# Last attention layer: first adjacency rows masked in the preparation, node softmax moved behind it, weights turned two chunks later

## The reference, cut to what matters

```
h = relu(layernorm(x))
node_att = softmax(h @ node_w, axis=0)         # one number per node, over all nodes
e = (h @ edge_w) @ (h @ edge_w).T              # 2708 x 2708 scores
e = where(adj > 0, e, -9e15)
edge_att = softmax(e, axis=1)
out = adj * (node_att * edge_att) @ (h @ weight) + bias
x = x + out
```

## Time and profile before

| what | value |
|---|---|
| time before, median of 3 runs | 2699.87 us (2698.82 to 2702.06) |
| profiled execution, its own time | 2702.05 us |
| its span | 2700.1 us |
| TensorE busy | 2484.8 us, 92% |
| VectorE busy | 1991.5 us, 74% |
| ScalarE busy | 1729.1 us, 64% |
| mean granted TensorE clock | 0.969 |

### The profile page before, as it was taken

How to read it: one execution, slowest core, us unless ns; L and a number is a source line. 1 busy time by engine, 2 the same in 40 slices (tenths; PEclk the granted TensorE clock), 3 DMA queues, 4 the chain that set the end, 5 groups by cost and what they waited for, 6 DMA issues and landing times. The chain is left out here.

```text
span 2700.1 us, 54411 instructions
## 1 busy us (share of the span) xinstructions
PE 2484.8 (92%) x20735; PEld 1537.6 (57%) x20735; DVE 1991.5 (74%) x3876; ACT 1729.1 (64%) x3162; POOL 40.5 (1%) x53
## 2 busy tenths in 40 slices
PE   7959999999999759999999995789989979999999
PEld 4524444444444339999999994334436735555554
DVE  5758999999997669999999986582246624455684
ACT  3438888888886558988888985851124544444542
POOL 1200000000000000000000000000000000000000
PEclk9979999999999879999999997999999989999999
DMA  4133334433331454111111114102211143434452
GB/s 179 33 113 124 129 138 143 156 129 129 132 120 72 168 179 177 40 39 41 39 29 39 39 28 176 71 23 68 81 52 40 39 133 96 117 109 130 125 141 52
DMA packets 186467, 261.02 MB, mean 97 GB/s; under 512 B 97161, under 2 KB 127689, under 8 KB 180485
## 3 DMA queue, kind: packets, MB, share of 16 engines
q1 hardware_dynamic: 180085, 229.25, 26.7%
q10 hardware_dynamic: 6160, 28.85, 3.3%
HBM read 198.45 MB, written 59.39 MB: 95 GB/s over the span
## 5 line engine op out<-in xcount | busy, mean ns | idle before, releaser
L1630 PE MATMUL m_acc<-m_y,m_b 128*128 128x260 f16 x3696 | 633.6, 275 | 21.9 <-DVE m_b L1416 20.5
L1633 PE MATMUL m_acc<-m_y,m_at 128*128 128x130 f16 x3696 | 630.4, 221 | 0.0
L1379 ACT ACTIVATE m_above<-m_u,m_nvs 128x512 bf16<-128x512 f32 (+1 forms) x864 | 519.6, 681 | 53.0 <-DVE m_b L1416 52.3
L1630 PEld LDWEIGHTS m_acc<-m_y,m_b 128*128 128x128 f16 x3696 | 359.6, 97 | 76.6 <-DMA m_at<-at 20.2
L986 PE MATMUL m_acc<-keep_z_hi,m_p_hi 128*128 128x512 f16 x968 | 362.1, 378 | 15.4 <-DVE m_p_lo L828 12.4
L1633 PEld LDWEIGHTS m_acc<-m_y,m_at 128*128 128x128 f16 x3696 | 363.8, 98 | 0.0
L989 PE MATMUL m_acc<-keep_z_lo,m_p_hi 128*128 128x512 f16 x924 | 349.9, 379 | 0.0
L991 PE MATMUL m_acc<-keep_z_hi,m_p_lo 128*128 128x512 f16 x924 | 348.7, 377 | 0.0
L1416 DVE TENSOR_TENSOR m_b<-m_above,m_at 128x1024 f16<-128x1024 bf16 (+1 forms) x432 | 278.1, 649 | 28.1 <-ACT m_above L1379 10.6
L722 ACT ACTIVATE m_p_hi<-m_pm 128x512 f16<-128x512 f32 x242 | 150.9, 623 | 88.0 <-DVE m_pm L820 81.0
L808 DVE TENSOR_TENSOR m_sc<-m_r,m_g_row 128x512 f32<-128x512 f32 x242 | 165.5, 684 | 21.4 <-DMA m_g_row<-part 17.2
(11 more groups left out here) (362 smaller groups left out, 5275.5 us busy)
## 6 DMA issues: line engine op xcount, KB each, us to landing
keep_a_rows<-adj ACTq DMA_DIRECT2D x40, 704.0 KB, 4.3
m_at<-adjT SPq DMA_DIRECT2D x11, 1408.0 KB, 8.5
at<-m_at SPq DMA_DIRECT2D x22, 704.0 KB, 3.9
keep_at_first<-at SPq DMA_DIRECT2D x22, 704.0 KB, 4.1
m_at<-adjT SPq DMA_DIRECT2D x11, 1280.0 KB
m_at<-at SPq DMA_DIRECT2D x5, 2816.0 KB, 16.8
m_u<-rows SPq DMA_DIRECT2D x40, 256.0 KB, 4.2
low<-m_lw SPq DMA_DIRECT2D x32, 256.0 KB, 5.4
```

The source lines that it names most:

```text
L1379: act.activation(pair(above, a % RA, nb)[:, i], u[:, g % RU, 0:nb], ACT.Relu, bias=nvs[:, k, 2 * p + i:2 * p + i + 1], scale=STEEP).then_i ...
L1630: pe.matmul(full.rearrange("p l y e -> p (l y e)"), pair(b01, (m // 2) % RB, nb)[:, m % 2, q // 2, half], y12[:, k % 2, j].rearrange("p l ...
L1633: last = pe.matmul(full[:, :, 1, :], at[:, i0 + q // 2, j, half], y2[:, k % 2, j], start=False, stop=(j == T - 2), skip_group_check=True)
```

## The change

- **First adjacency rows.** `prep3` loads rows 0 to 127 of the adjacency behind the store of its third chunk of x, into the first tiles of `rel`, which are no longer read. ScalarE masks them in two halves, ahead of steps 14 and 16 of the pipeline, into a new tile `am0`. `attention3` has no `load_mask(0)` and no `mask(0)`; `upper(0, c)` reads `am0`, and the first load issued is `load_mask(1)`.
- **Node softmax.** Its operations leave `prep3`. In `attention3` its maximum stands behind `upper(0, 0)`, its subtraction behind `upper(0, 2)`, its exponential on ScalarE behind `exp_upper(0)`, and its last part on VectorE (`node_factors`) ahead of `weight(0)`. The small load `valid` moves with it, between `load_mask(1)` and the load of `bias`.
- **Turns.** For block 0, `after_chunk` is 2, 3, 4.

```diff
@@ prep3
+        nl, am0 = keep["nl"], keep["am0"]
+        a0, HALF = rel[:, 0:6, :].rearrange("p t d -> p (t d)")[:, 0:N], N // 2
...
-                sp.dma_start(valid[:], dram["valid"]).then_inc(v_in, 16)
                 for c, (t0, n) in enumerate(CHUNKS):
                     sp.wait_ge(x_made, t0 + n)
                     sp.dma_start(tiles(dram["x3"])[:, t0:t0 + n, :], x_all[:, t0:t0 + n, :]).then_inc(x_out, 16)
+                    if c == 2:
+                        sp.dma_start(a0, dram["adj"][0:P, 0:N]).then_inc(a0_in, 16)
...
-                pool.partition_all_reduce(gmall, gm, P, RMAX).then_inc(m_all, 1)
...
+                def mask_first(n):
+                    act.wait_ge(a0_in, 16)
+                    of = slice(n * HALF, (n + 1) * HALF)
+                    act.activation(am0[:, of], a0[:, of], ACT.Copy, scale=BIG, bias=-BIG).then_inc(a0_made, 1)
...
-                         before=[(2 * n, lambda n=n: answer(n)) for n in range(4)])
-                act.wait_ge(asked, 1)
-                act.activation(ne[:], nl[:], ACT.Exp, accum_out=gz).then_inc(answered, 1)
+                         before=[(2 * n, lambda n=n: answer(n)) for n in range(4)] + [(14 + 2 * n, lambda n=n: mask_first(n)) for n in range(2)])
+                act.wait_ge(a0_made, 2)
...
-                ch.scale(valid[:], valid[:], BIG, ALU.mult, -BIG, ALU.add)
...
-                ch.fused(node[:], ne[:], gzall, nl[:], ALU.mult, ALU.mult)
@@ attention3
+            if t == 0:
+                return [2 + g for g in range(len(GROUPS[t]))]
             return [min(2 * g, last) for g in range(len(GROUPS[t]))]
...
-                load_mask(0)
+                sp.sem_inc(a_in, 16)
+                load_mask(1)
+                sp.dma_start(valid[:], dram["valid"]).then_inc(v_in, 16)
                 sp.dma_start(bias[:], dram["bias3"].broadcast_to([P, D])).then_inc(bias_in, 16)
-                load_mask(1)
                 load_x(0)
...
                 pool.memset(w_hi[:, N:NP], 0.0).then_inc(tail_made, 1)
+                pool.wait_ge(m_made, 1)
+                pool.partition_all_reduce(gmall, gm, P, RMAX).then_inc(m_all, 1)
+                pool.wait_ge(z_made, 1)
+                pool.partition_all_reduce(gzall, gz, P, RADD).then_inc(z_all, 1)
...
                 dve.wait_ge(bias_in, 16)
                 for c in range(len(EC[0])):
                     upper(0, c)
+                    if c == 0:
+                        node_maximum()
+                    if c == 2:
+                        node_shift()
...
+                        if t == 0:
+                            node_factors()
                         weight(t)
...
-                mask(0)
+                act.sem_inc(am_made, 1)
                 for c in range(len(EC[0])):
                     evacuate(0, c)
                     if c == 0:
                         mask(1)
                 exp_upper(0)
+                act.wait_ge(node_link, 1)
+                act.activation(ne[:], nl[:], ACT.Exp, accum_out=gz).then_inc(z_made, 1)
```

More of the change, by code:

```diff
@@ L2154, in prep3 @@
         std, rstd, nmr = kit.sb("std", [2]), kit.sb("rstd", [2]), kit.sb("nmr", [2])
-        valid, nl, ne = kit.sb("valid", [T]), kit.sb("nl", [T]), kit.sb("ne", [T])
-        one = kit.sb("one", [4, 1])
+        nl, am0 = keep["nl"], keep["am0"]
+        a0, HALF = rel[:, 0:6, :].rearrange("p t d -> p (t d)")[:, 0:N], N // 2
         tp = kit.ps("tp", [2, KC, P])
@@ L2160, in prep3 @@
         small = kit.ps("small", [2, 256])
-        s_hi, s_lo, e_hi, e_lo, node = (keep[n] for n in ("s_hi", "s_lo", "e_hi", "e_lo", "node"))
+        s_hi, s_lo, e_hi, e_lo = (keep[n] for n in ("s_hi", "s_lo", "e_hi", "e_lo"))
         s = dict(zip("stats mv var std rstd nmr".split(), kit.sems("stats mv var std rstd nmr")))
         late_link, late_asked, late_answered = kit.sems("late_link late_asked late_answered")
[L2164 to L2168, removed]
+        (gate, a0_in, a0_made, x_made, x_out, h_ready, tp_ready, hi_ready, lo_done, prod_done, s_hi_made, s_lo_done,
+         e_hi_made, e_lo_done, nl_done) = kit.sems(
+            "gate a0_in a0_made x_made x_out h_ready tp_ready hi_ready lo_done prod_done s_hi_made s_lo_done "
+            "e_hi_made e_lo_done nl_done")
         with nc.Block() as block:
@@ L2276, in _ @@
                 dve.wait_ge(nl_done, done(T - 1))
-                dve.wait_ge(v_in, 16)
-                ch = Chain(dve, link, asked, answered)
-                ch.scale(valid[:], valid[:], BIG, ALU.mult, -BIG, ALU.add)
[L2281 to L2289, removed]
-                ch.fused(node[:], ne[:], gzall, nl[:], ALU.mult, ALU.mult)
         kit.close()
@@ L2314, in attention3 @@
         x, bias = kit.sb("x", [RX, D]), kit.sb("bias", [D])
+        valid, ne, one = kit.sb("valid", [T]), kit.sb("ne", [T]), kit.sb("one", [4, 1])
+        gm, gmall, gz, gzall = (one[:, i, :] for i in range(4))
         sc = kit.ps("sc", [SB, CW])
@@ L2318, in attention3 @@
         misc = kit.ps("misc", [512])
-        s_hi, s_lo, e_hi, e_lo, node = (keep[n] for n in ("s_hi", "s_lo", "e_hi", "e_lo", "node"))
+        s_hi, s_lo, e_hi, e_lo, node, nl, am0 = (keep[n] for n in ("s_hi", "s_lo", "e_hi", "e_lo", "node", "nl", "am0"))
         x_in, l_in, l_out, out_done = (kit.sems(" ".join(f"{n}{i}" for i in range(r)))
@@ L2581, in upper @@
                     dve.wait_ge(sc_made, q + 1)
-                    dve.tensor_tensor_reduce(emf[0:r, b, n0:n0 + n], sc[0:r, q % SB, 0:n], amf[0:r, b, n0:n0 + n], 1.0, -3e38,
+                    added_mask = am0[:, n0:n0 + n] if t == 0 else amf[0:r, b, n0:n0 + n]
+                    dve.tensor_tensor_reduce(emf[0:r, b, n0:n0 + n], sc[0:r, q % SB, 0:n], added_mask, 1.0, -3e38,
                                              ALU.add, ALU.max, mx[0:r, b, c + 1:c + 2]).then_inc(tt_made, 1)
@@ L2676, in finish, with node_maximum, node_shift, node_factors @@
                     dve.tensor_tensor(x[0:r, i, :], x[0:r, i, :], bias[0:r, :], ALU.add).then_inc(fin_made, 1)
+                def node_maximum():
+                    dve.wait_ge(v_in, 16)
+                    dve.tensor_scalar(valid[:], valid[:], BIG, -BIG, ALU.mult, ALU.add).then_inc(v_link, 1)
+                    dve.wait_ge(v_link, 1)
+                    dve.tensor_tensor(nl[:], nl[:], valid[:], ALU.add).then_inc(v_link, 1)
+                    dve.wait_ge(v_link, 2)
+                    dve.tensor_reduce(gm, nl[:], AXX, ALU.max).then_inc(m_made, 1)
+                def node_shift():
+                    dve.wait_ge(m_all, 1)
+                    dve.tensor_scalar(nl[:], nl[:], gmall, None, ALU.subtract).then_inc(node_link, 1)
+                def node_factors():
+                    dve.wait_ge(z_all, 1)
+                    dve.reciprocal(gzall, gzall).then_inc(v_link, 1)
+                    dve.tensor_scalar(valid[:], keep["iso"][:], -1.0, 1.0, ALU.mult, ALU.add).then_inc(v_link, 1)
+                    dve.wait_ge(v_link, 4)
+                    dve.scalar_tensor_tensor(node[:], ne[:], gzall, valid[:], ALU.mult, ALU.mult).then_inc(v_link, 1)
+                    dve.wait_ge(v_link, 5)
                 dve.wait_ge(bias_in, 16)
@@ L2836, in build @@
             keep |= {n: kit.sb(n, [KC, NP], F16) for n in ("e_hi", "e_lo")}
-            keep["node"] = kit.sb("node", [T])
+            keep |= {"node": kit.sb("node", [T]), "nl": kit.sb("nl", [T]), "am0": kit.sb("am0", [N], BF16)}
             prep3(nc, dram, keep)
```

9 lines of the change are left out of this document (2 added, 7 removed).

## The result

| what | before | after |
|---|---|---|
| median of 10 runs | 2700.7 us | 2693.07 us (2692.07 to 2695.35) |
| ratio | | 0.9972, 95% interval 0.9963 to 0.998 |
| profiled execution, its own time | 2702.05 us | 2692.31 us |
| its span | 2700.1 us | 2690.2 us |

The change gained 7.6 us. The direction was as forecast; the size was not: 14.0 us were expected, and the median lies outside the range of 2684.2 to 2690.0 us.

What follows compares the result with a forecast made beforehand. TensorE was taken as the bound, so only the start of its long busy stretch counts: 2.9 + 11.8 - 0.7 = 14.0 us less, a median of 2685.9 us. The range was 2684.2 to 2690.0 us.

Steps and rivals of the forecast that it cites:

- Softmax out of the preparation: At the border, VectorE's last preparation operation ends earlier without the node softmax: 2.9 us gained, TensorE's hole 3.1 us.
- First `upper`: VectorE's start in the attention: waits for `bias`, starting 6.7 us after TensorE's first matmul instead of 8.5.
- Exponential behind the table load: On ScalarE after block 0's last evacuations: with 1.3 us for the table load, the exponential starts at t = 17.5.
- First turn: TensorE's first turn, 8.39 us after the exponential starts: t = 25.9 instead of 32.7, behind 3.0 us idle.
- Second turn: TensorE waits 2.0 us for ScalarE's `move`, standing behind `mask(2)` and two evacuations: t = 31.6.
- Turns later: Block 0's turns on TensorE: last small chunk at t = 35.7 instead of 47.5, 11.8 us gained; list worth 3 us.
- the clock: TensorE around the first turn: a clock drop at t = 23 costs 1.1 us at most; 0.7 us taken.
- The sum for the old list: Block 0 with the old turn list: the last small chunk would begin at about t = 38.7.
- 1 (the queue holds the start): Attention's start: `bias` lands at t = 9.5 to 10; gain 11.6 us, 2688.3 us; chance 0.12.
- 2 (twice the load's row): Chain to the exponential: table switch costs 2 x 1.28 us; gain 12.7 us, 2687.2 us; chance 0.13.
- 3 (the holes only move): TensorE still waits, moves behind `mask(2)` late for block 2's rows; gain 9 us, 2690.9 us; chance 0.08, including similar losses.
- 4 (slower): Preparation: loop cuts at steps 14 and 16 hold ScalarE, stopping TensorE; median above 2705.3 us; chance 0.03.

Runs made afterwards that it cites:

- e8: Changed kernel with one dummy exponential ahead of the first evacuation of `attention3`, so the table loads while ScalarE idles; 2689.83 us, 0.9958 of before.
- e1: Kernel before with only the new turn list (2, 3, 4) for block 0; 2700.32 us, 0.9998 of before.
- e2: Changed kernel with block 0's turns behind chunks 0, 2, 4 again; 2694.96 us, 0.9969 of before.
- e5: Changed kernel with four instead of three buffers of `lw`; 2689.11 us, 0.9948 of before.
- e6: Changed kernel with the store of chunk (1,0) issued ahead of block 3's adjacency rows; 2688.70 us, 0.9945 of before.
- e9: Changed kernel with chunk (1,0)'s store ahead of block 3's rows and the exponential's table loaded early; 2686.46 us, 0.9939 of before.
- e10: Changed kernel with early table, `mask(2)` behind the first `move`, and block 3's rows issued behind three stores; 2684.42 us, 0.9934 of before.

## Why the prediction missed, step by step

**Held, with their sizes.** *Softmax out of the preparation*: 2.9 us forecast, 3.19 measured, the hole 2.83 us (3.1). *Half masks*: 1.34 us each (1.25), hidden: the preparation is no longer than before. TensorE is busy for 79.76 of the same 80 us. *First `upper`*: 7.12 (6.7). *No hole before chunk 4*: none. *Exponential behind the table load*: starts at t = 17.67 (17.5). The Trainium skill (ScalarE: Activation LUTs, What ACT_TABLE_LOAD costs) would add a drain of 1.38 us to the load; the traces do not agree: 1.28 us for its row, 1.47 us when it was taken away (e8). *First turn*: 26.05 (25.9), its hole 2.71 (3.0). *Second turn*: 31.66 (31.6). The clock did fall behind the first turn, and from the start of chunk (1,3) to the second turn 4.42 us passed instead of the 2.59 of a chunk at full clock; the 1.83 us vanished in the wait for the move, as the step said, so the 2.0 us hole has no row. *Softmax in its new place, node factors*: hidden.

**The step that failed** is *Turns later*: "Then the second turn 0.9, chunk (1,4) 2.6, third turn 0.6 us". It lets the third turn go without a wait. It needs the second `move`, and this stands behind `evacuate(1, 3)` on ScalarE, which waits for a store. Before, the second turn came behind chunk (1,2), so its move stood ahead of `evacuate(1, 3)`, and this evacuation, at 2220.13, waited for nothing but its chunk; a wait for the store there would not have held up the second turn's move. I read that row for its length and not for what it might wait for in another order. I followed ScalarE's order for `mask(2)` and the first two evacuations only, and worked out for no evacuation when its buffer of `lw` comes free. Rows of before alone would have given the hole, as an estimate: by the forecast `mask(2)` ends at t = 29.6; before, the store was issued 0.87 us behind that point (2212.27 to 2213.14) and landed 6.1 us later, so t = 36.6; with 0.5 us to the move and 1.0 us for it the third turn starts at 38.1, where the forecast has TensorE ready at 35.1: 3.0 us, as measured. Shown: e1 has the wait with the list alone, e2 loses it without the list, e5 and e6 remove it in two unlike ways.

**The second miss is where the clock was priced.** I asked only whether it falls at t = 23, where a wait absorbs it, and took 0.7 us. It fell there at no cost, and again in the third hole, with `products(0)` right behind. Third turn: 1.15 us to the last small chunk instead of 0.61; rest: 2.44 us more.

Together: 3.0 (hole) + 0.5 (slow third turn) + 2.4 (slow start of `products(0)`) = 5.9, less the 0.7 allowed for, is 5.2 us too much. 14.0 - 5.2 = 8.8, against the 8.74 us between the traces. That this comes out so closely is in part luck, since the 2.4 is the value of this trace and others have 1.2 to 1.7. The medians give 7.6; the executions of after alone lie 3.3 us apart, and that last 1.1 us has no row.

**With the failed step cured, the sum stands.** The last small chunk at 35.53 and 35.77 (e5, e6), forecast 35.7; 15.0 and 14.8 us from `e_lo`, 14.4 and 14.8 us between medians, forecast 14.0 (14.7 without the 0.7 us for the clock, which cost nothing there). What the list is worth, 3 us by the forecast, is -0.75 as built, and by these two 5.3 to 5.5 us against e2, which has neither cure but no wait that either would remove.

**A third miss is in what the list is worth.** The sum for the old list, 38.7, prices the stretch behind its hole of 8.2 us at full clock. In e2, behind a hole of 7.89 us, 8.35 us pass from the first to the second turn instead of 6.1, and the last small chunk comes at 41.05. Before had shown it: 14.75 us from its first turn to its last small chunk, where the sum has 12.8.

**The rivals.** 1 (the queue holds the start): 7.12 excludes `bias` at 9.5. 2 (twice the load's row): excluded by e8. 3 (the holes only move) was right in kind, a late landing on ScalarE's way to a move; its place was wrong. The rows of block 2 were there, and `mask(2)` did not wait. Its chance of 0.08 was too small. 4 (slower): nothing of it.

**The chances do not add up to the last line.** With half of rival 3's 0.08 and the 0.03 for no visible change counted as "same", that is 0.07 and "faster" 0.90, not 0.04 and 0.93.

## What to carry to other kernels

When an action moves later in an engine's fixed order, write down every instruction that now stands ahead of it, and for each which buffer it writes and what frees that: here a ring of three, freed by a store, whose place in a shared DMA queue was set by a load that has nothing to do with it. A drop of the clock costs nothing if a wait follows that is longer than what it delays, and its full amount if the long busy stretch follows (here 1.2 to 2.4 us from trace to trace); price each hole by what stands behind it. A change that gains less than its sum says may hide a new wait worth as much again: here one load issued behind one store instead of ahead of it took the gain from 7.6 to 14.8 us.

## What the runs showed of the hardware that was not expected

**The same store, 1.8 or 6.1 us.** 128 KB landed 6.1 us after the issue when issued behind 1216 KB in the same queue (before, after), and 1.8 us after it when issued ahead of them (e6).

**An all-reduce on GpSimd of 0.38 or 2.95 us.** The first two rows and the last are of after, the third is of before, columns as in the timelines above:

```profile
2179.00 0.38 POOL L2457 PARTITION_ALL_REDUCE m_one<-m_one  x1 [8.28 <-DVE m_one L2679]
2193.78 2.95 POOL L2459 PARTITION_ALL_REDUCE m_one<-m_one  x1 [14.39 <-ACT m_ne L2807]
```
```profile
2172.61 0.40 POOL L2186 PARTITION_ALL_REDUCE p_one<-p_one  x1 [0.77 <-ACT p_ne L2216]
```
```profile
2193.51 2.96 DVE L2656 TENSOR_TENSOR m_w_lo<-m_em,m_w_hi 128x2688 f16<-128x2688 f32 x1 [6.35 <-ACT m_w_hi L2781]
```

The second one of after, also on a single column, begins 0.27 us after VectorE's `w_lo` and ends 0.26 us after it. The Trainium skill (GPSIMD Engine Reference, Specifications) says that GpSimd shares its SBUF interfaces with VectorE, with contention when VectorE reads two SBUF inputs, as `w_lo` does; the rows agree with it. The first one takes the maximum and the second the sum, but that is not the difference: the row of before is the same sum, at a place where no `w_lo` runs, and took 0.40 us. That it is the interfaces, and not something else about running beside `w_lo`, is argued and not shown. Nothing waited for it: the result is read at 2210.80.

**The clock and the holes.** A hole of 3.02 us left TensorE at a granted clock of 0.50 for the 5.3 us behind it. With holes of 1.28 and 1.65 us and none longer (e9), or 1.28 alone (e10), there was no matmul at the lower level between the first turn and `products(0)`. How long a slow stretch lasts does not follow from the hole ahead of it: behind 3.02 us (after) the slow start of `products(0)` cost 2.44 us, behind 3.33 us (e1) 1.24 us.
